# Joining attention and experts in one block, with the first expert batch routed inside attention's last batch

## The reference, cut to what matters

```python
mod = (_silu(L0_c) @ L0_wmod).reshape(16, 6, 1, -1)         # sa, ca, ga, sb, cb, gb
h = _layernorm(x) * (1 + ca) + sa
x = x + ga * attention(h)          # causal softmax, 16 heads of 64, then W_out and b_out
h = _layernorm(x) * (1 + cb) + sb
logits = h @ Wr + br               # 8 experts; softmax over the best two, others get weight 0
hid = gelu(einsum('td,edh->eth', h, W1) + b1)               # 128 -> 512 in every expert
expert_out = einsum('eth,ehd->etd', hid, W2) + b2           # 512 -> 128
x = x + gb * einsum('etd,te->td', expert_out, weights)
```

## Time and profile before

| What | Value |
|---|---|
| Time, median of 3 runs | 2023.12 us (2021.97 to 2023.38) |
| The profiled execution's own time | 2025.12 us |
| Its span, first to last instruction | 2023.3 us |
| TensorE busy | 1979.4 us (98%) |
| VectorE / ScalarE / GpSimd busy | 1694.6 / 1582.1 / 737.8 us |
| Mean granted TensorE clock | 0.993 of full speed |

### The profile page before, as it was taken

One profiled execution on the slowest core, in us unless ns is written; L12 is line 12 of the kernel. 1 busy time (PEld: TensorE's weight loads), 2 busy tenths in 40 slices (PEclk: granted clock), 3 DMA queues, 4 the chain that ended last, 5 costly groups with the idle time before them and its releaser, 6 DMA issues. The chain is left out here.

```text
span 2023.3 us, 46361 instructions
## 1 busy us (share of the span) xinstructions
PE 1979.4 (98%) x12703; PEld 1543.2 (76%) x12703; DVE 1694.6 (84%) x4518; ACT 1582.1 (78%) x3765; POOL 737.8 (36%) x1214
## 2 busy tenths in 40 slices
PE   6999999999999999999999998799999999999998
PEld 5777777777777777777777776578888888888886
DVE  6887888888888887888888876799999999999997
ACT  5888888888888888888888886677777777777775
POOL 3444444444444444444444444122222222222222
PEclk9999999999999999999999999899999999999999
DMA  4000000000000000000000000311121111111120
GB/s 128 7 2 0 0 0 0 0 0 0 0 0 0 0 0 0 0 0 0 0 0 0 0 1 1 125 48 47 54 75 54 47 47 52 47 47 47 48 75 24
DMA packets 42252, 49.46 MB, mean 24 GB/s; under 512 B 3112, under 2 KB 24160, under 8 KB 42208
## 3 DMA queue, kind: packets, MB, share of 16 engines
q1 hardware_dynamic: 41952, 48.41, 7.5%
q0 software_dynamic: 256, 0.53, 0.1%
HBM read 44.47 MB, written 4.46 MB: 24 GB/s over the span
## 5 line engine op out<-in xcount | busy, mean ns | idle before, releaser
L285 POOL TENSOR_SCALAR probs<-probs,rdenom 128x512 f32<-128x512 f32 (+3 forms) x1024 | 524.8, 538 | 699.0 <-DVE rdenom L690 699.0
L542 ACT ACTIVATE probs<-probs,neg_max 128x256 f32<-128x256 f32 (+3 forms) x1024 | 567.9, 555 | 72.9 <-DVE neg_max L681 70.8
L681 DVE CUSTOM_DVE_ANT_0 probs<-banks,mask_w 128x256 f32<-128x256 f32 (+3 forms) x1024 | 435.0, 481 | 84.4 <-PE banks L347 82.9
L1060 ACT ACTIVATE hidden<-banks,b_cols 128x512 f32<-128x512 f32 x512 | 348.8, 686 | 194.6 <-PE banks L926 191.7
L1176 DVE TENSOR_TENSOR hid_lo<-hidden,hid_hi 128x512 fp32r<-128x512 f32 x512 | 379.4, 751 | 52.5 <-ACT hid_hi L1068 39.4
L373 PE MATMUL banks<-ident,probs 128*128 128x128 f32 x2560 | 340.6, 276 | 3.3 <-POOL probs L285 2.3
L674 DVE COPY probs_T<-banks 128x512 f32<-128x512 f32 x384 | 258.4, 687 | 91.1 <-PE banks L373 91.0
L1000 POOL TENSOR_TENSOR acc<-acc,y_w 128x512 f32<-128x512 f32 x112 | 159.5, 1424 | 467.7 <-DVE y_w L1189 467.7
L373 PEld LDWEIGHTS banks<-ident,probs 128*128 128x128 f32 x2560 | 288.9, 141 | 49.2 <-DVE neg_max L681 19.2
L388 PE MATMUL banks<-probs_T,v_sb 128*64 128x512 f32 (+3 forms) x2048 | 303.9, 439 | 1.6 <-DVE probs_T L674 1.6
L388 PEld LDWEIGHTS banks<-probs_T,v_sb 128*64 128x64 f32 x2048 | 135.5, 136 | 148.5 <-issue 119.0
(11 more groups left out here) (140 smaller groups left out, 3377.2 us busy)
## 6 DMA issues: line engine op xcount, KB each, us to landing
w_rows<-w_kept SPq DMA_DIRECT2D x128, 256.0 KB, 3.9
x_all<-in_L_attn_resid_dram SPq DMA_DIRECT2D x16, 256.0 KB, 2.6
out_dram<-y_result SPq DMA_DIRECT2D x16, 256.0 KB, 2.4
w_raw<-in_L_ffn_W_dram SPq DMA_DIRECT2D x12, 256.0 KB, 5.1
hidden<-in_L_ffn_W_dram SPq DMA_DIRECT2D x4, 256.0 KB, 6.2
v_sb<-in_L_attn_W_Q_dram SPq DMA_DIRECT2D x1, 512.0 KB, 5.7
v_sb<-in_L_attn_W_K_dram SPq DMA_DIRECT2D x1, 512.0 KB, 6.5
v_sb<-in_L_attn_W_V_dram SPq DMA_DIRECT2D x1, 512.0 KB, 7.8
```

The source lines that it names most:

```text
L285: pool.tensor_scalar(part, part, rdenom[:, p % 2, 4 * h + r:4 * h + r + 1], 1.0, ALU.mult, ALU.mult)\
L542: act.activation(part, part, ACT.Exp, bias=neg_max[:, p % 2, col:col + 1], scale=-1.0, accum_out=denom[:, p % 2, col:col + 1]).then_inc(p_ ...
L681: dve.tensor_tensor_reduce(out=probs[:, p % 2, h, at:at + n], in0=S_BANK[u][h][:, col:col + n], in1=mask_w[:, 512 - n:512], scale=-SCALE, ...
L1060: act.activation(hidden[:, e % 2, c, :], banks[:, c, :], ACT.Gelu, bias=b1_cols[:, e * HC + c:e * HC + c + 1]).then_inc(hid, 1)
```

## The change

The two blocks become one. The experts' large tensors are placed at the addresses of attention's, in an order in which each attention tensor is dead when its successor is first written; `w_raw` (the raw weights) and the router's small tensors get memory of their own, and the experts use attention's `h_hi` and `h_lo`. In the places of attention's last batch that were empty, batch 0 of the experts is normalized and routed. Its first expert layers are mixed into attention's tail.

- **SP**: after the loads of x the eight loads of W1 are issued at once. A W2 load waits until the split of the same expert's W1 has freed its part of `w_raw`. `lay_weights` of batch 0 stands behind the first two W2 loads, and the other six stand behind it.
- **POOL**: `router_inv_std(0)` at step 2 of attention's last batch; after the last `probs` scaling it makes the rests of W1 of experts 4 to 7, and in expert batch 0 those of W2 of experts 4 to 7, each behind an `add_expert`. Before, DVE made all sixteen.
- **PE, DVE, ACT**: see the core of the diff.

```diff
 # PE, attention's body
+ if p == 5 and last: pe.wait_ge(s_masked, pair(8, b, p) + 8); norm_T(0, s_banks[3])
+ if p == 6 and last: pe.wait_ge(r_full, 1)
+ if p == 7 and last: pe.wait_ge(s_masked, pair(8, b, p) + 8); router_logits(0, s_banks[2])
 # PE, attention's tail
  weigh_values(end, NP - 2)
- for u in range(5):
-     transposes(end, NP - 1, u, False)
+ transposes(end, NP - 1, 0, False)
+ transposes(end, NP - 1, 1, False)
+ pe.wait_ge(r_lo, 1)
+ wait_split(pe, 1, 0)
+ first_chunk(0, 0, 0, True)
+ first_chunk(0, 0, 1, True)
+ transposes(end, NP - 1, 2, False)
+ transposes(end, NP - 1, 3, False)
+ transposes(end, NP - 1, 4, False)
+ weights_T(0, s_banks[2])
+ pe.wait_ge(t_act, pair(2, end, NP - 1) + 1)
+ first_chunk(0, 0, 2, True)
  weigh_values(end, NP - 1)
+ first_chunk(0, 0, 3, True)
+ wait_split(pe, 1, 1)
+ first_chunk(0, 1, 0, False)
+ first_chunk(0, 1, 1, False)
  project_out(end, 1, pair(8, end, NP))
+ first_chunk(0, 1, 2, False)
+ first_chunk(0, 1, 3, False)
  attention_T(end, None)
 # PE, experts: batch 0 begins with second_layer(0, 0); before second_layer(0, 1) it waits for x_mid
 # ACT, step 7 of the last batch, ahead of evac_T, and the tail
+ round_w(1, 0); round_w(1, 1)
...
+ for e in range(2, 7): round_w(1, e)
  round_z(B - 1, NP - 2)
+ logit_exp(0)
  evac_T(B - 1, NP - 1, 1, False)
+ round_w(1, 7)
  evac_T(B - 1, NP - 1, 3, False)
+ weights_out(0, s_banks[2])
+ round_w(2, 0)
+ hidden_chunk(0, 0, 0, True)
+ hidden_chunk(0, 0, 1, True)
  round_z(B - 1, NP - 1)
+ hidden_chunk(0, 0, 2, True); round_chunk(0, 0, 0, True)
+ hidden_chunk(0, 0, 3, True); round_chunk(0, 0, 1, True)
+ act.wait_ge(o_ps, 2 * B)
 # DVE, last batch: norm_stats(0) at p=2, norm_rows(0) at p=3 and 4, router_rest_h(0) at p=6,
 # and at p=7, ahead of the two evac_T:
+ split_expert(1, 0); split_expert(1, 1)
 # DVE, tail
  invert_sums(end, NP - 1)
+ choose(0, s_banks[2][:, 0:NT * E])
+ evac_T(end, NP - 1, 0, False)
  rest_z(end, NP - 2)
- for u in (0, 2, 4):
-     evac_T(end, NP - 1, u, False)
+ weights(0)
+ evac_T(end, NP - 1, 2, False)
+ evac_T(end, NP - 1, 4, False)
+ split_expert(1, 2); split_expert(1, 3)
  rest_z(end, NP - 1)
+ split_expert(2, 0)
+ for c in range(HC): rest_chunk(0, 0, c, True)
  gate_attention(end)
- add_attention(end)
 # DVE, experts' batch 0, e = 1: split_expert(2, 1), rest_chunk c=0 and 1, add_attention(end), c=2 and 3
 # POOL, behind its last batch of attention, and in the experts' batch 0
+ for e in range(HC, E): split_expert(1, e)
...
+ pool.wait_ge(oT_ps, B)
+ add_expert(b, e); if 2 <= e < HC + 2: split_expert(2, e + 2)
```

More of the change, by code:

```diff
@@ L169, in adaln_moe_kernel @@
+            y_out, stored = sem("y_out"), sem("stored")
             load_c, load_b = sem("load_c"), sem("load_b")
@@ L289, in _, with experts @@
                     batches(pool, body)
+                    for e in range(HC, E):
+                        split_expert(1, e)
+                    def experts(b, first, last):
+                        if not first:
+                            add_expert(b - 1, E - 1)
+                        if not last:
+                            router_inv_std(b + 1)
+                        if first:
+                            pool.wait_ge(oT_ps, B)
+                        for e in range(1, E - 1):
+                            add_expert(b, e)
+                            if first and 2 <= e < HC + 2:
+                                split_expert(2, e + 2)
+                    batches(pool, experts)
+                    add_expert(B - 1, E - 1)
                 @block.tensor
@@ L507, in _ @@
+                    batches(pe, experts)
+                    second_layer(B - 1, E - 1, False)
+                    sum_T(B - 1)
                 @block.scalar
@@ L764, in _ @@
                     dve.tensor_copy(b2_cols[:, :], g_bank[:, 64:64 + E]).then_inc(b_ok, 1)
[L766 to L793, removed]
-                            if has_next:
-                                rest_q(*nxt)
-                            if has_next:
-                                rest_k(*nxt)
-                            if not begin:
-                                evac_T(*prev, 2, False)
-                                evac_T(*prev, 4, False)
-                            if p == 4 and not first:
-                                add_attention(b - 1)
-                            if p == 6 and not last:
-                                rest_h(b + 1)
-                            if p == 2 and not first:
-                                gate_attention(b - 1)
-                            if begin:
-                                split_weights(3)
@@ L1202, in body, with experts @@
+                    split_expert(2, 0)
+                    for c in range(HC):
+                        rest_chunk(0, 0, c, True)
+                    gate_attention(end)
+                    def experts(b, first, last):
                         for e in range(E):
                             young = first and e < 2
-                            if first:
-                                for other in (range(HC) if e == 1 else (e + 2,) if HC <= e + 2 < E else ()):
-                                    split_w(E + other, 2, other)
+                            if first and 1 <= e < HC:
+                                split_expert(2, e)
```

670 lines of the change are left out of this document (364 added, 306 removed).

## The result

| | before | after |
|---|---|---|
| Median of 4 runs each | 2023.25 us (2021.97 to 2023.53) | 2001.09 us (2000.17 to 2002.11) |
| Profiled execution, its span | 2025.12 us, 2023.3 us | 2000.88 us, 1999.1 us |
| Mean granted clock | 0.993 | 0.998 |

The ratio is 0.989 [0.9879, 0.9902]: 22.2 us faster, where 20.5 were forecast and 2002.6 us predicted. The page's first line of after stands against the earlier trace rows: TensorE lost 12.1 us of busy time although it has the same instructions. Removing waits alone would leave the busy time as it was. So I looked for two more things beside the waits: a higher clock, and matmuls that start closer together.

A forecast was written before the change was run, and what follows sets the result against it. TensorE, busy 1979.4 of 2023.3 us, was taken as the bound. 22.65 us gained up to expert 4, less 1.4 for DVE's lag and 0.7 for hand-overs, gives 20.5: from 2023.1 to 2002.6 us, range 1998.5 to 2011.

The forecast's parts named there:

- Up to expert 4: From attention's last steps to expert 4's first layer in batch 0: starts at 1281.65 instead of 1304.30, gaining 22.65 us.
- Step 7's wait: Step 7 of attention's last batch: TensorE gaps of about 1 us remain there.
- the logits' price: Eight logit matmuls in step 7 of attention's last batch, priced at 0.95 us.
- The end of batch 0: Expert batch 0: DVE some 1.8 us later, 1.4 us on the path; small hand-overs in the tail cost another 0.7.
- rival 1: Expert batch 0: POOL's splits make DVE the bound, 3 to 7 us more, 2005.5 to 2010 us; chance 0.17.
- POOL beside DVE: Experts 4 to 7: POOL's four late splits hit DVE's rests, costing DVE between 0 and 4.4 us, taken as 3.6.
- rule of full blocking: Skill's lock-out of DVE and GpSimd: four late splits cost DVE 1.54 each, 6.2 us; forecast 2.6 us later, about 2005.2.
- The tail's four: POOL's four splits in attention's tail: DVE loses 0.6 and about 1.3 us, and rest_z is late by 0.35.
- The rest lies at the kernel's two ends, which the diff leaves alone: Of at most 43.9 us winnable, 21.6 us lie between attention and experts; the remainder, at both ends, is untouched.
- Rival 2: W2 loads or routing weights land late; cover 0.3 us on ACT, price beyond 1.7; 2006 to 2012 us; chance 0.09.
- Rival 3: DVE's lead holds, both late waits vanish, hand-overs cost nothing: gain 23.75 us, 1999.4 us; chance 0.07.
- Rival 4: Tail's short waits bring TensorE to 1.2 GHz and keep it there, slower than before, 2026 us; chance 0.015.

The follow-up runs named there:

- experiment 1: Changed kernel with TensorE's wait for expert 7's last W2 rest moved behind the first layer of batch 1: 1999.93 us, ratio 0.9886.
- experiment 2: Changed kernel with the W2 rests of experts 4 to 7 made by DVE at the start of its steps instead of POOL: 1998.97 us, ratio 0.9882.
- experiment 8: Changed kernel with experiment 1's wait, late W2 rests on DVE at its steps' ends, POOL's four W1 rests held until routing weights are ready: 1999.89 us.
- experiment 4: Kernel before with only the allocation order of attention's tensors changed to that of the changed kernel: 2019.87 us, ratio 0.9985.
- experiment 6: Kernel before with only the 4-byte-wide bo_col allocated behind attention's other tensors: 2019.5 us, ratio 0.9982.
- experiment 9: Changed kernel with experiment 1's wait, experiment 8's POOL order, DVE making W2 rests of experts 4 to 6 at step start, 7 at step end: 1997.55 us.
- experiment 3: Changed kernel with expert chunks not mixed into attention's tail, TensorE finishing attention first, ACT and DVE reordered to match: 2010.92 us, ratio 0.9939.
- experiment 11: Kernel before with an unused 4-byte-wide tensor ahead of wq, moving weights one pad and everything behind bo_col a second: 2021.88 us, ratio 0.9994.
- experiment 12: Changed kernel with an unused 4-byte-wide tensor ahead of h_hi, moving only h_hi, h_lo and what lies behind them: 2012.86 us, ratio 0.9948.
- experiment 5: Changed kernel run again, unchanged, for its scatter: 2002.33 us, ratio 0.9898.
- experiment 10: Changed kernel with unused 4-byte-wide tensors ahead of wq and w1_hi, moving all large tensors one pad further: 2000.02 us, ratio 0.9882.
- experiment 7: Changed kernel with experiment 1's wait and DVE making the W2 rests of experts 4 to 7 at the end of its steps: 2001.07 us, ratio 0.9893.

## Why the prediction was right, and where not

**Up to expert 4: right, and by its own steps.** Forecast 22.65 us, measured 22.73. That the end agrees to 0.1 is in part luck, since steps on the way were off by up to 0.7. With the 6.0 us of lead taken off, the forecast start of `weigh_values` of pair 6 is 1244.35 (measured 1244.18), of pair 7 1251.65 (1252.31), of `project_out` 1256.1 (1256.79), of second_layer of expert 0 1261.3 (1261.50), of expert 4 1275.65 (1275.57). The errors cancel: the routing weights were 0.4 late, since DVE's `kept` took 1.38 us beside POOL's rests where the same instruction takes 0.18 elsewhere, but the wait for attn_T was 0.2 instead of 0.55, and the five layers behind it took 0.3 less than their price. Step 7's wait stayed (1.03 where 1.0 was forecast), and the logits' price was right (0.96 for 0.95).

**The end of batch 0: right mechanism, wrong size, and one wait in the wrong place.** I put 1.4 us on the path and named waits for w_now of 0.8 and for h_lo of 1.8. They were 1.08 and, once the wait ahead of it was out of the way, 1.70 (experiment 1). What the sum lacked is that TensorE asks for the last rest of W2 at the end of step 7, that POOL delivers it 1.1 us after h_lo, and that the clock is halved behind the wait of 3.03. The term was 2.95 + 1.6 = 4.55 instead of 1.4 + 0.7, and the clock in it was not in the forecast at all. "3 us and more is rival 1" would have named the wrong remedy: experiment 1, which takes nothing off DVE, removes 2.9 of it. But rival 1 is true in part. POOL's last rest came late because its addition waited for DVE's y_w, and with the four rests back on DVE (experiment 2) w_now comes in time, the 3.03 us wait goes too, and 3.7 us come back.

**POOL beside DVE.** The four late rests lengthened DVE's CAST (1.51 for 0.42), `chosen` (1.32 where the instruction ahead of it, of the same width, took 0.25), the pair at 1294.08 (2.43 for 1.3) and the rest at 1301.49 (1.74 for 0.69): 4.3 us, just under the upper end of 4.4 that I had given, where I took 3.6. The Trainium skill, "SBUF — State Buffer", section "Who interferes with whom", also lists casts among what can contend with GpSimd; the CAST of 1.51 agrees with that. But of the 6.2 us that the prediction worked out by its rule of full blocking, the rows show 4.3, and the measurement decides. The tail's four cost TensorE about 1 us of waits (0.77 and 0.22, gone in experiment 8 against a new one of 0.30), in place of the 0.35 that I had put on the path.

**"The rest lies at the kernel's two ends, which the diff leaves alone": wrong for attention, and it hid the shortfall.** This is the step that failed, beside the size of the last term. Two things differ outside the stretch that the sum covers. First, attention gained about 3 us because the new list of allocations no longer has bo_col ahead of q_hi2 (experiments 4 and 6). Second, the start: the profiled execution of before has a low clock there,

```profile
32.00:36.00 4.00, 2.68 (x12) 2.20 (x12) 2.71 (x11) 2.52 (x9) 3.71 (x8) 0.50 0.28 82
```
and after does not:
```profile
32.00:36.00 4.00, 3.74 (x24) 3.27 (x25) 2.69 (x8) 3.33 (x10) 2.23 (x5) 1.00 0.28 79
```

That gave 3.2 us at 40 us, but the other kernels have leads of 0.1 to 3.2 there, whether they carry the change or not. I read it as scatter between executions and not as a gain; the profiled execution of before was also 1.9 us above its median, and the medians differ by 22.2 where the spans differ by 24.2. Only one execution of each kernel has a trace, so this is argued and not shown. So of 22.2 some 18.2 are the change's moves and about 3 the addresses; the remaining 1 lies within the scatter. My 20.5 was 2.3 too much for the moves, and the addresses, which were not in my sum, made up for it: that the total came within 1.5 us of 2002.6 is luck as far as those two go.

**Rival 2** did not decide, but its thin cover was used up. ACT in after:

```profile
1264.84 0.64 ACT L910 ACTIVATE w_hi<-w_raw 128x512 fp32r<-128x512 f32 x1 [1.15 <-DMA w_raw<-in_L_ffn_W_dram]
```

1.15 of the 1.7 us, and TensorE did not wait. **Rival 3**'s size was reached by experiment 9 (23.6 behind step 7, forecast 23.75). **Rival 4** fell here; experiment 3 shows it in small.

**Open**: why a shift between the two operands of a matmul costs 6 to 8 ns, why some kinds of matmul go the other way, why experiment 11 kept only 2.0 of before's 3.4 us, and why the second layer slowed down in experiment 12. Also why the same 3.0 us wait is followed by the lower clock in after, in experiments 3, 5 and 12, and not in experiment 10.

## What to carry to other kernels

Moving work into places where the bound engine is busy anyway pays what the gaps say, and a layout of instruction starts, written out, predicted it to 0.1 us at its end and 0.7 on the way; the larger errors were in what stood outside it. A wait belongs ahead of the instruction that needs it, not at the end of the step before, and work given to POOL is charged to DVE where their instructions meet. When buffers are rearranged, compare the distances of matmuls in a stretch without waits before and after: a tensor of 4 bytes can shift all the others, and cost or bring 3 to 10 us of 2000.

## What the hardware showed that I had not expected

- A tensor of 4 bytes per partition between the weights and the other tensors of attention made hi·lo matmuls start 0.2333 to 0.2336 us apart instead of 0.2265 to 0.2271, at a granted clock of 1.00: 3.4 us in 1200. Shifting everything alike (experiment 10) cost nothing; shifting h and what lies behind it (experiment 12) cost 10.0 us behind step 7, about 4 of them in matmuls whose operands had not moved.
- The granted clock halved after waits of 1.04, 0.93 and 0.92 us with short work between (experiment 3), and after single ones of 2.07 and 1.81 (experiments 7 and 8), which cost 3.4 and twice 1.7 us. It did not after waits of 0.94, 0.78 and 1.42 in the kernel before, after a single one of 1.78 (experiment 2), or after one of 3.02 (experiment 10).
- The clock of the first 40 us differed between executions of kernels with the same start, worth up to 3 us.
- A DVE instruction of 0.18 us took 1.38 beside a POOL TENSOR_TENSOR.
